# Mamba layer with a mixture of experts on one core: the first expert four slots earlier, its residual reordered, z moved to the stage's end, sixteen filler matmuls taken out

## What is computed

```python
def mamba(x):                                  # L0_attn, D_INNER=512, 16 states, 4 taps
    x_in, z = split(x @ W_in)                  # 512 + 512 channels
    u = silu(causal_conv(x_in, conv_w) + conv_b)
    dt, B, C = split(u @ W_xproj)              # 16, 16, 16
    delta = softplus(dt @ W_dt + b_dt)
    h_t = exp(delta * A) * h_{t-1} + delta * u * B     # per channel and state
    y = sum_n h_t[n] * C[n] + D_skip * u
    return (y * silu(z)) @ W_out
def ffn(x):                                    # 8 experts of 128, top 2, shared of 256
    coef = top2(softmax(x @ router))           # others are 0
    routed = sum_e coef[e] * (silu(x @ gate[e]) * (x @ up[e])) @ down[e]
    return routed + (silu(x @ shared_gate) * (x @ shared_up)) @ shared_down
x = x + layernorm(mamba(layernorm(x)))
return x + layernorm(ffn(layernorm(x)))        # every expert is computed for every token
```

## Time and profile before

| | |
|---|---|
| median of three runs | 2650.46 us (2644.72 to 2653.87) |
| profiled execution | 2651.34 us, of which 2649.6 us from the first to the last instruction |
| DVE busy | 2267.9 us (86%) |
| PE busy | 2276.8 us (86%) |
| POOL busy | 1864.8 us (70%) |
| ACT busy | 1627.5 us (61%) |
| mean granted PE clock | 0.94 of full |

### The profile page before, as it was taken

One profiled execution on the slowest core, in us unless ns is written; L12 is line 12 of the kernel. 1 busy time (PEld: TensorE's weight loads), 2 busy tenths in 40 slices (PEclk: granted clock), 3 DMA queues, 4 the chain that ended last, 5 costly groups with the idle time before them and its releaser, 6 DMA issues. The chain is left out here.

```text
span 2649.6 us, 30782 instructions
## 1 busy us (share of the span) xinstructions
PE 2276.8 (86%) x9472; PEld 1419.5 (54%) x9472; DVE 2267.9 (86%) x3240; ACT 1627.5 (61%) x2418; POOL 1864.8 (70%) x1534
## 2 busy tenths in 40 slices
PE   5779989899898988989898898989889898897877
PEld 2345655555555555555555555555555555565544
DVE  2898898989899898898989889898989889898950
ACT  4556657567675766757576675756667576674531
POOL 2575876958678695877858587794967769587733
PEclk9859989999999999999999999999999899997989
DMA  4101211211112111211111121121111111121101
GB/s 114 41 32 40 61 52 45 68 33 52 48 53 60 41 56 37 64 50 55 60 35 52 47 61 52 47 66 33 52 52 52 57 41 46 39 64 48 55 22 40
DMA packets 92948, 134.30 MB, mean 51 GB/s; under 512 B 12000, under 2 KB 42976, under 8 KB 92784
## 3 DMA queue, kind: packets, MB, share of 16 engines
q1 hardware_dynamic: 92784, 132.34, 16.9%
HBM read 123.13 MB, written 9.18 MB: 50 GB/s over the span
## 5 line engine op out<-in xcount | busy, mean ns | idle before, releaser
L748 DVE TENSOR_TENSOR_SCAN h<-d_a,carry,d_bu 128x512 f32<-128x512 f32 x1024 | 1301.9, 1274 | 56.1 <-ACT d_a L590 54.1
L986 POOL TENSOR_TENSOR d_bu<-delta_u,b_rows 128x1024 f32<-128x1024 f32 x512 | 1202.7, 2358 | 5.0 <-DMA b_rows<-b_rows_hbm 0.9
L590 ACT ACTIVATE d_a<-delta,a_neg 128x512 f32<-128x512 f32 x1024 | 698.9, 689 | 758.1 <-DVE h L748 753.5
L447 PE MATMUL ht<-ident,h 128*128 128x128 f32 x4096 | 667.0, 295 | 248.2 <-DVE y_t L758 222.8
L447 PEld LDWEIGHTS ht<-ident,h 128*128 128x128 f32 x4096 | 520.1, 151 | 616.4 <-issue 307.7
L758 DVE SCALAR_TENSOR_TENSOR y_t<-ht,c_t,y_t 128x512 f32<-128x512 f32 x960 | 701.3, 732 | 90.4 <-PE ht L447 88.0
L1023 POOL TENSOR_TENSOR carry<-h,one 128x4 f32<-128x4 f32 x256 | 51.3, 201 | 555.2 <-DVE h L748 555.2
L526 PE MATMUL dn<-w_down_sb,hidden 128*128 128x256 f32 x1280 | 317.2, 392 | 33.6 <-POOL hidden L1042 30.5
L506 PE MATMUL ring<-x_t,w_up_sb 128*128 128x512 f32 x640 | 304.2, 599 | 7.5 <-ACT silu_gate L666 5.7
L499 PE MATMUL ring<-x_t,w_gate_sb 128*128 128x512 f32 x640 | 305.2, 601 | 0.0
L526 PEld LDWEIGHTS dn<-w_down_sb,hidden 128*128 128x128 f32 x1280 | 236.1, 194 | 80.2 <-POOL hidden L1042 53.2
(11 more groups left out here) (108 smaller groups left out, 2089.5 us busy)
## 6 DMA issues: line engine op xcount, KB each, us to landing
b_rows<-b_rows_hbm SPq DMA_DIRECT2D x256, 256.0 KB, 3.4
coef_rows<-coef_rows_hbm SPq DMA_DIRECT2D x128, 256.0 KB, 3.5
xa<-L_attn_x_in SPq DMA_DIRECT2D x16, 512.0 KB, 3.9
xr<-L_attn_x_in SPq DMA_DIRECT2D x16, 512.0 KB, 3.8
out<-xr SPq DMA_DIRECT2D x16, 512.0 KB, 2.9
w_in_sb<-L_attn_W_in_in SPq DMA_DIRECT2D x1, 1024.0 KB, 6.2
w_gate_sb<-L_ffn_experts_gate_in SPq DMA_DIRECT2D x2, 512.0 KB, 5.2
w_up_sb<-L_ffn_experts_up_in SPq DMA_DIRECT2D x2, 512.0 KB, 5.8
```

Source lines behind the costliest of these rows:

```text
L447: last = nc.tensor.transpose(HT[q % HTS][:, j * P:(j + 1) * P], H[:, (NS * c + n) % HS, j, a * P:(a + 1) * P], IDN[:, :])
L590: nc.scalar.activation(DA[i % DAS][:, :], DL[:, r, j, :], ACT.Exp, scale=ANEG[:, j, n:n + 1]).then_inc(ex.sem, 1)
L748: nc.vector.tensor_tensor_scan(H[:, (NS * s + n) % HS, j, :], DA[(n * J + j) % DAS][:, :], BU[:, (2 * n + j // 2) % 4, j % 2, :], CARRY[:, ...
L986: nc.gpsimd.tensor_tensor(BU[:, (2 * n + h) % 4, :, :], DU[:, 2 * h:2 * h + 2, :], BB[:, n % 2, :].unsqueeze(1).to_broadcast([P, 2, T]), A ...
```

## The change

Seven edits, which come together:

1. All 16 `keep_warm` matmuls go.
2. `shifted_stream` goes. XR stays as loaded, `add_stream_o` adds o/sigma to it, so x1 lacks o's mean/sigma; the layernorm of x1 is not affected by that per-token constant, and POOL adds it to the final shift (`rstd_of("y")` has one more small multiply-add step).
3. The four y transposes sit in slot 3, in four banks (both ring banks and both dn banks); the four `skip_u` in slot 4, the four `gate_y` in slot 5, the four `project_out` in slots 6 and 7.
4. The chain behind them moves up: moments of o in slots 9 and 10, residual and moments of x1 in 11, `normed` in 13, x1 transposes in 13, first gate in 15.
5. The z products go from slots 12 to 18 to slots 57, 58, 60, 61, their silu from 15 and 19 to 59 and 62; they are last in `RING_USE`.
6. Pairs of experts come every nine slots: g is 15, 24, 33, 42, 51; xd, cf, ct, dl and softplus move up by one to four slots.
7. `rstd_of("y")` goes from slot 1 of the next stage to slot 62 of this one, the final residual from slot 3 to 1, its shift from 4 to 3, the output store and the load of XR two slots up; the moments of y are all in slot 61.

```diff
-        XIN_PE, TAP0_ACT = (6, 6, 9, 11), (7, 8, 10, 12)
-        TAP = ((8, 8, 8), (9, 9, 9), (11, 11, 11), (13, 13, 13))
-        YD_PE, YD_DVE, Y_GATE, OUT_PE = (3, 3, 4, 4), (4, 4, 5, 5), (5, 5, 6, 6), 7
-        Z_PE = (12, 14, 17, 18)
-        SILU = {11: [("u", 0), ("u", 1)], 15: [("u", 2), ("u", 3), ("z", 0), ("z", 1)], 19: [("z", 2), ("z", 3)]}
-        X1T_PE, GATE_PE = 18, 19
-        XD_PE, CF_PE, CT_PE = 24, 25, 48
-        DL_PE, DL_ACT = (32, 33, 40, 41), (34, 34, 42, 42)
+        XIN_PE, TAP0_ACT, CONV = (5, 5, 8, 9), (6, 7, 9, 10), (7, 8, 10, 12)
+        YD_PE, YD_DVE, Y_GATE, OUT_PE = 3, 4, 5, (6, 6, 7, 7)
+        X1T_PE, GATE_PE, PAIR = 13, 15, 9
+        XD_PE, CF_PE, CT_PE = 20, 21, 47
+        DL_PE, DL_ACT = (29, 30, 38, 39), (31, 31, 40, 40)
...
+        Z_PE = (57, 58, 60, 61)
+        SILU = {9: [("u", 0), ("u", 1)], 14: [("u", 2), ("u", 3)], 59: [("z", 0), ("z", 1)], 62: [("z", 2), ("z", 3)]}
...
         def gate_slot(f):
-            return GATE_PE + 8 * (f // 2) + f % 2
+            return GATE_PE + PAIR * (f // 2) + f % 2
...
             def x_in(s, lo, j):
...
-                keep_warm(ring_bank("xin", j))
...
-                pe.wait_ge(*ring_user_before(s, lo, "yd", j))
-                bank = ring_bank("yd", j)
+                if j < 2:
+                    pe.wait_ge(*ring_user_before(s, lo, "yd", j))
+                else:
+                    pe.wait_ge(resid["y"].sem, resid["y"].at(s - 2))
+                bank = yd_bank(j)
...
             def add_stream_o(c, a):
 
-                dve.wait_ge(stream["o"].sem, stream["o"].at(c, a + 1))
+                dve.wait_ge(xr_ld.sem, xr_ld.at(c))
+                dve.wait_ge(rstd["o"].sem, rstd["o"].at(c))
                 nc.vector.scalar_tensor_tensor(XR[:, a, :], dn(a), RS["o"][:, a:a + 1], XR[:, a, :],
-                                               ALU.mult, ALU.subtract).then_inc(resid["o"].sem, 1)
+                                               ALU.mult, ALU.add).then_inc(resid["o"].sem, 1)
...
+                if w == "y":
+                    pool.wait_ge(shift["y"].sem, shift["y"].at(c, 1))
+                    pool.wait_ge(shift["o"].sem, shift["o"].at(c))
+                    nc.gpsimd.tensor_tensor(MR["y"][:, :], MR["y"][:, :], MR["o"][:, :], ALU.add)\
+                      .then_inc(shift["y"].sem, 1)
...
-                    if exists(lo - 2) and t == 1:
-                        rstd_of("y", s - 2)
...
+                    if ffn and t == 62:
+                        rstd_of("y", s - 1)
...
-                if t == X1T_PE - 1:
+                if t == X1T_PE:
                     normed("x1", c, XN, XR)
```

More of the change, by code:

```diff
@@ L162, in mamba_moe_kernel @@
         tap0 = stage("tap0", J)
-        shift = {w: stage(f"shift_{w}", 1 if w == "o" else 2) for w in ("xa", "o", "x1", "y")}
-        stream = {w: stage(f"stream_{w}", NT) for w in ("o", "y")}
+        shift = {w: stage(f"shift_{w}", n) for w, n in dict(xa=2, o=1, x1=2, y=3).items()}
+        stream = stage("stream", NT)
         scan, add_c, carry = stage("scan", NS * J), stage("add_c", (NS - 1) * NT), stage("carry_s", NS)
@@ L354, in body @@
                         sp.dma_start(XA[:, :, :], following).then_inc(xa_ld.sem, 16)
-                    if exists(lo - 2) and t == 5:
-                        result, added = tokens(out, r, half - 1), stream["y"].at(s - 2)
-                        sp.wait_ge(stream["y"].sem, added)
+                    if exists(lo - 2) and t == 3:
+                        result, added = tokens(out, r, half - 1), stream.at(s - 2)
+                        sp.wait_ge(stream.sem, added)
                         sp.dma_start(result, XR[:, :, :]).then_inc(out_st.sem, 16)
-                    if ffn and t == 6:
+                    if ffn and t == 4:
                         again, stored = tokens(x, 1 - r, half + r - 1), out_st.at(s - 2)
@@ L422, in x_t @@
                     last.then_inc(full["xt"].sem, 1)
-            def keep_warm(bank):
-                nc.tensor.matmul(bank[:, :], IDN[:, :], WIN[:, 0, 0:T], start=True, stop=True)
             def x_in(s, lo, j):
@@ L469, in ffn_part @@
                 c = s - 1
[L470 to L471 removed]
+                if t == YD_PE:
+                    for j in range(J):
                         transpose_y(s, lo, j)
[L473 to L477 removed]
+                for a in range(NT):
+                    if t == OUT_PE[a]:
+                        pe.wait_ge(y_gate.sem, y_gate.at(c))
+                        pe.wait_ge(resid["y"].sem, resid["y"].at(c - 1, 2 * (a // 2) + 2))
+                        project_out(c, a)
                 if t == X1T_PE:
@@ L609, in normed @@
                       .then_inc(norm[w].sem, 1)
-            def shifted_stream(c):
-                act.wait_ge(xr_ld.sem, xr_ld.at(c))
-                act.wait_ge(shift["o"].sem, shift["o"].at(c))
-                for a in range(NT):
-                    nc.scalar.activation(XR[:, a, :], XR[:, a, :], ACT.Identity,
-                                         bias=MR["o"][:, a:a + 1], scale=-1.0).then_inc(stream["o"].sem, 1)
             def shift_result(c):
@@ L637, in body @@
                         first_state(s, r, t - NT - 1)
-                    if exists(lo - 2) and t == 4:
+                    if exists(lo - 2) and t == 3:
                         shift_result(s - 2)
@@ L818, in result_part @@
             def result_part(c, t):
-                if t == 3:
+                if t == 1:
                     for a in range(NT):
@@ L869, in ffn_part @@
             def ffn_part(c, o, t):
-                for j in range(J):
-                    if t == YD_DVE[j]:
+                if t == YD_DVE:
+                    for j in range(J):
                         skip_u(c, o, j)
-                if t in (10, 12):
-                    a = 0 if t == 10 else 2
+                if t in (9, 10):
+                    a = 2 * t - 18
                     dve.wait_ge(o_full.sem, o_full.at(c, a + 2))
@@ L1000, in body @@
                         inflow(s, n + 1, t % NT // 2)
-                    if exists(lo - 2) and t == 1:
-                        rstd_of("y", s - 2)
-                    for j in range(J):
-                        if ffn and t == Y_GATE[j]:
+                    if ffn and t == 62:
+                        rstd_of("y", s - 1)
+                    if ffn and t == Y_GATE:
+                        for j in range(J):
                             gate_y(s - 1, o, j)
-                    if ffn and t == 12:
+                    if ffn and t == 10:
                         rstd_of("o", s - 1)
-                    if ffn and t == 16:
+                    if ffn and t == 11:
                         rstd_of("x1", s - 1)
```

61 lines of the change are left out of this document (20 added, 41 removed).

## The result

| | median | against the kernel before, same chip |
|---|---|---|
| kernel before | 2648.81 us (2644.72 to 2653.87) | 1 |
| changed kernel | 2657.11 us (2654.17 to 2658.66) | 1.003, interval 1.0018 to 1.0041 |

The median is 8.3 us or 0.3% longer, which lies just at the line that the prediction drew between "same" and "slower" (8 us). The profiled execution took 2654.39 us, 2652.6 of it between the first and the last instruction. The forecast was 2654 for a profiled execution and 2652 for the median, so the total was right.

The account below looks back on a forecast made before the run. DVE's work was the floor of a stage, with 15.1 us of waits to win. 15 stages x (+0.4 - 0.3) = +1.5 and ends +1.5: 2651.3 + 3 = 2654 us profiled, 2652 median; range 2608 to 2694, likeliest case 2630 to 2674.

Parts of the forecast that it names:

- The sum over a stage: DVE's waits per stage: slots 0 to 20 +0.4 us (8.7 against 8.3), slots 21 to 61 -0.3 (6.45 against 6.8).
- tap 0: ACT's convolution tap, late for slot 7 as it was for slot 8: DVE waits 0.95 us.
- Slot 9's 0.75: DVE's slot 9 waits 0.75 us for PE's transposes, behind x_in and output groups.
- Hidden 7: Slot 48: POOL's hidden 7 stands behind inflow and rstd of xa, so down 7 is late; DVE waits 2.4 us.
- clock at the expert pairs: Rival: PE's clock falls waiting for hidden 7; down 7, gates 8 and 9 at half speed, +45 us, 2697; chance 0.14.
- signs of being wrong: Stage waits under 13.5 or over 17 us, low clock between expert pairs, or x_in not finding the full clock.
- Transposes warm PE: Slot 3's y transposes restore the clock; the rival says they do not, slot 9 waits 3 longer, +45 us; chance 0.07.
- Fillers out: Fillers leaving PE, 16.8 us a stage, gain no time in themselves, as PE idles elsewhere; the clock can fall.
- The shift: Removing ACT's shift, 1.7 us a stage, saves nothing in slots 0 to 20; ACT's order sets the slot of `normed`.
- Pairs every nine slots: Slots 21 to 61: no slot holds both down and next gate, so two waits, about 2 us a stage, go.
- The same kind of wait, 1.27 on PE, is there today without harm: Expert pairs: PE's present wait of 1.27 us is harmless, and the clock there is 1.00.
- The ends: Prologue -1.5 us; behind the last scan +3 (between -3 and +7), from lower-clock output and router products; together +1.5.

Follow-up runs that it names:

- three places: Changed kernel with rstd of xa in slot 49, four fillers ahead of the x1 transposes and the router's exp a slot earlier: together 2571.74 us.
- the last version: Changed kernel with rstd of xa in slot 49, four x1 fillers, router's exp a slot earlier, and silu of u behind the gates': 2550.70 us, ratio 0.9625.
- x1's fillers: Changed kernel with four filler matmuls put back in PE's slots 12 and 13, ahead of the x1 transposes: 2628.16 us.
- the run with the router's exp: Changed kernel with the router's exp one slot earlier in ACT's order, nothing else: 2629.69 us.
- the one with rstd in slot 49: Changed kernel with POOL's rstd of xa moved from slot 48 to 49, behind hidden 7: 2632.19 us.

## Why the prediction came out as it did

**The sum over a stage, right, in part by luck.** Each wait was worked out in the new order from the queues, and most of the terms hold: scan 1 0.8 (measured 0.85), tap 0 0.95 (0.93), slot 15 2.3 (1.97), scan 17 1.5 (1.66), the router's exp 1.15 (1.26), exps of slots 28 and 33 0.85 and 1.05 (0.85 and 1.03), of slots 37 and 42 0.85 and 1.05 (0.6 with slot 36, and 0.93). Slot 9's 0.75 did not come: the two x_in end 17.3 after the stage's start, where 19 was forecast. The 0.2 in the sum is given no source, and slots 1 to 6 show no such wait. Slots 0 to 20 have 7.7 in all, where 8.7 was forecast; slots 21 to 63 have 7.7, where 6.45 was (or 6.3, as the 0.15 for exp is in the 2.4 and counted again). The two errors, 1.0 and 1.25 a stage or 15 and 19 us in all, have opposite signs and cancel.

**Hidden 7, right in kind and short in size.** Forecast were 2.4 for slots 52 to 54 and a bound of 3 more for a lower clock. At the full clock the stages of the other runs show 2.0 + 0.21 + 0.21 = 2.4. In the changed kernel it was 3.47 + 0.22 + 0.21 = 3.9, because down 7 ran at the lower clock. The rival "clock at the expert pairs" came true for one of its three groups: 1.5 us in each of 15 stages, 22 us, where it had 45. So one of the prediction's signs of being wrong came true, "above all if the clock is low between the expert pairs": the granted clock is 0.50 from 1260.7 to 1264.1. The other did not; the sum of the waits, 15.4, lies between its 13.5 and 17.

**Transposes warm PE, right.** The y transposes of slot 3 stand in the stretch at 0.50 that ends at 1144.6, with only transposes before them on PE; behind it the clock is 1.00 and the two x_in take 3.60, full speed. The rival fell. The Trainium skill's sentence on this ("TensorE: Matmul & The Clock Gate", section on the PE-mode transpose) says that the full clock does not engage for transposes, as they do not count as busy in the same way; in this stage the trace does not agree, for transposes of float32.

**Fillers out, wrong.** The step "That is no gain of time in itself: PE idles elsewhere" failed. Taking them out gained 34 us in the kernel before, and eight of the sixteen, those at x_in and z, cost 48 to 52 in either kernel. PE did idle, but not between the x_in and the state transposes behind it, and ACT's tap 0 stood in its queue behind a `first_state` that needed these transposes. The prediction had the wait (the 0.93 and "two more like it") and its releaser ACT, and did not follow the releaser one step further back.

**The shift, wrong.** "Saves nothing here, since ACT's order, not its work, sets the slot of `normed`" failed as well: 18.6 us in the changed kernel. What it would have delayed first was not `normed` but DVE's addition (1.19 a stage), which the change had moved to one slot behind the moments.

**Why the total stood all the same.** The waits of before were read from the trace and those of after were forecast nearly right as a sum, so their difference was right; the assignment to the parts of the change was not. The runs give a path from one kernel to the other: all fillers out is 34.2 below the kernel before, the new order with the shift still in place and no fillers (the run with ACT's shift put back) is 26.9 above it, and without the shift the time is 8.3 above. So the new order costs 26.9 + 34.2 = 61 us once the fillers are gone; taken in another sequence the parts can come out differently. 86 us lay in three places that a small edit each takes away.

**Pairs every nine slots, wrong.** "With nine slots no slot has two such groups [...] so both waits go": they did go, but with pairs every eight in the changed kernel they do not come back either. So the distance was not needed for it. The step that failed is that the shared slot alone costs 2 us; by the traces PE also has to come late to it. "The same kind of wait, 1.27 on PE, is there today without harm" fails with it: that wait stands ahead of the 2.04 of slot 53.

**The ends.** Forecast were -1.5 and +3, measured -6.5 and +10.7, which miss by 5.0 and 7.7 in opposite directions and leave 4.2 where 1.5 was forecast. Why the prologue gained so much was not tried. In the tail the lower clock is behind the projection (9.8 instead of 7.1); what lies behind the last scan grew by 6.8 (118.2, was 111.4), just inside the bound of +7, and the last stage, for which the sum had no term of its own, by 3.9 more. The 15 distances between stages are 1.2 shorter, where +1.5 was forecast.

## What to carry to other kernels

A wait's named releaser may itself be queued behind something: follow it back until an engine that was busy, and count there what the change puts in or takes out, warm-up matmuls too. A warm-up pays where PE is idle and what follows is on the path (four ahead of the x1 transposes: -31 us), and costs time in front of a group that PE has to fit between two sets of transposes (eight a stage, 6.9 us of PE: +50 in all, 3.2 a stage). When a large reordering leaves the time as it was, repair its new waits one by one: they added up here, and the last version is 100 us below the kernel before. And take each part of a change out by itself in the old kernel too: the cheapest gain here, 52 us, was eight fillers out and nothing moved.

## What the runs showed of the hardware

The lower clock is not bound to one place. The same kernel pays for it in slot 17 in one stage and in slot 52 in the next, 1.5 to 2.7 us each time. Two fillers that kept down 7 at full speed moved the time by 5 us of 22, as slot 17 then waited in every second stage. Edits at another place (x1's fillers, the router's exp) shifted slots 17 and 52 by 0.2 to 0.7 a stage, and executions of the run with the router's exp spread by 12 us, of the one with rstd in slot 49 by 26. A single stage is then a poor sample: the means over stages 2 to 14 told these runs apart.

A table load of ACT takes 1.28 us, and the function behind it starts 1.29 to 1.30 after the load's start (1180.71 to 1182.00 and 1183.17 to 1184.47 in stage 7 of the changed kernel; 334 of its 340 loads are followed within 1.35). The Trainium skill ("ScalarE: Activation LUTs", section "What ACT_TABLE_LOAD costs") gives the same load, 1283 ns, but adds a drain of about as much; in this kernel no such second half shows.
